# Keys pass of a linear-attention block: products one group later, three shared PSUM banks, sums folded at the end of a batch

## What is computed

```
q, k, v = xn Wq, xn Wk, xn Wv                       16 heads of 32
pq, pk  = exp(u.omega - |u|^2/2 - max(u.omega)) / sqrt(128) + 1e-6     u = scaled q or k, 128 features
kv      = sum over the rows of a batch of pk^T v     per head 128 x 32
z       = sum over the rows of a batch of pk         per head 128
out     = (pq kv) / (pq z) Wo
```

## Time and profile before

| | |
|---|---|
| median of 3 runs | 3785.38 us (3782.58 to 3794.86) |
| the profiled execution's own time | 3801.29 us |
| its span | 3799.5 us |
| granted TensorE clock, mean | 0.968 |
| busy: PE, PEld | 3564.6 us (94%), 3134.4 us (82%) |
| busy: DVE, ACT, POOL | 2196.7 us (58%), 1838.1 us (48%), 1416.3 us (37%) |
| keys pass | 0 to 984 us |
| attend pass | 984 to about 2270 us |
| feed-forward pass | to the end |

### The profile page before, as it was taken

How to read it: one execution, slowest core, us unless ns; L and a number is a source line. 1 busy time by engine, 2 the same in 40 slices (tenths; PEclk the granted TensorE clock), 3 DMA queues, 4 the chain that set the end, 5 groups by cost and what they waited for, 6 DMA issues and landing times. The chain is left out here.

```text
span 3799.5 us, 74203 instructions
## 1 busy us (share of the span) xinstructions
PE 3564.6 (94%) x27634; PEld 3134.4 (82%) x27634; DVE 2196.7 (58%) x3304; ACT 1838.1 (48%) x3944; POOL 1416.3 (37%) x954
## 2 busy tenths in 40 slices
PE   7989988898599999999999968999999999999998
PEld 6777777777488888888888857898898889998897
DVE  5777776677477777877878744333333333333332
ACT  5767766676355555655656534323223222333322
POOL 2544544454344444544445431222222222222222
PEclk9999999999699999999999988999999999999999
DMA  2221232212323232222332324111111111111111
GB/s 95 100 91 67 86 104 85 85 67 90 106 86 102 91 97 94 93 91 92 96 97 92 99 68 145 44 44 44 44 44 44 44 44 44 44 44 44 44 45 49
DMA packets 162443, 283.82 MB, mean 75 GB/s; under 512 B 23696, under 2 KB 52880, under 8 KB 161168
## 3 DMA queue, kind: packets, MB, share of 16 engines
q1 hardware_dynamic: 162192, 280.42, 21.8%
HBM read 166.08 MB, written 114.29 MB: 74 GB/s over the span
## 5 line engine op out<-in xcount | busy, mean ns | idle before, releaser
L1444 DVE TENSOR_TENSOR ffn_hT_lo<-ffn_hid,ffn_hT_hi 128x512 fp32r<-128x512 f32 x256 | 334.3, 1334 | 492.5 <-ACT ffn_hT_hi L1420 492.5
L96 PE MATMUL ffn_hidden<-ffn_yT_hi,ffn_wa_hi 128*128 128x256 f32 x2048 | 573.5, 280 | 11.9 <-DVE ffn_yT_lo L1440 11.9
L96 PE MATMUL ffn_hidden<-ffn_yT_hi,ffn_wa_lo 128*128 128x256 f32 x2048 | 573.6, 280 | 0.0
L96 PE MATMUL ffn_hidden<-ffn_yT_lo,ffn_wa_hi 128*128 128x256 f32 x2048 | 572.6, 280 | 0.0
L1411 ACT ACTIVATE ffn_hid<-ffn_hidden,ffn_bias 128x256 f32<-128x256 f32 x512 | 213.7, 468 | 669.0 <-PE ffn_hidden L96 646.3
L232 POOL TENSOR_TENSOR ffn_n_rstd<-ffn_n_base,ffn_n_power 128x2 f32<-128x2 f32 x32 | 22.5, 702 | 1072.6 <-DVE ffn_n_negmean L227 1072.6
L96 PE MATMUL ffn_result<-ffn_wb_hi,ffn_hT_hi 128*128 128x512 f32 x1024 | 412.0, 402 | 2.4 <-DVE ffn_hT_lo L1444 2.2
L96 PE MATMUL ffn_result<-ffn_wb_hi,ffn_hT_lo 128*128 128x512 f32 x1024 | 404.5, 395 | 0.0
L96 PE MATMUL ffn_result<-ffn_wb_lo,ffn_hT_hi 128*128 128x512 f32 x1024 | 404.2, 395 | 0.0
L96 PEld LDWEIGHTS ffn_hidden<-ffn_yT_hi,ffn_wa_hi 128*128 128x128 f32 x2048 | 384.9, 188 | 20.9 <-DVE ffn_yT_lo L1440 12.2
L96 PEld LDWEIGHTS ffn_hidden<-ffn_yT_lo,ffn_wa_hi 128*128 128x128 f32 x2048 | 385.2, 188 | 8.9
(11 more groups left out here) (229 smaller groups left out, 10112.3 us busy)
## 6 DMA issues: line engine op xcount, KB each, us to landing
attend_uq<-u_d SPq DMA_DIRECT2D x33, 512.0 KB, 3.6
ffn_y_in<-y_d SPq DMA_DIRECT2D x33, 512.0 KB, 3.7
keys_xin<-in_L_attn_x_dram SPq DMA_DIRECT2D x32, 512.0 KB, 5.6
xn_d<-keys_xn SPq DMA_DIRECT2D x32, 512.0 KB, 4.9
xT_d<-keys_xT_whole SPq DMA_DIRECT2D x32, 512.0 KB, 2.7
u_d<-keys_uq SPq DMA_DIRECT2D x32, 512.0 KB, 3.5
attend_xTf<-xT_d SPq DMA_DIRECT2D x32, 512.0 KB, 5.4
r_d<-attend_gate SPq DMA_DIRECT2D x32, 512.0 KB, 2.8
```

The source lines that it names most:

```text
L96: last = pe.matmul(out, stationary[a], moving[b], start=start and n == 0, stop=stop and n == len(TERMS) - 1)
L1444: dve.tensor_tensor(hT[n % HB].lo[:, :, :], hid[n % 2][:, :, :], f32(hT[n % HB].hi[:, :, :]), ALU.subtract).then_inc(h_ready[n % HB], 1)
```

## The change

1. **Ring.** dense0, dense1 and kv go; three banks, ring0 to ring2, serve k, q, v and kv in a fixed rotation.
2. **One group later.** kv of a group runs in the body of the next group, between the dense jobs.
3. **xT in two buffers**, so turn_x of g + 2 no longer waits for the dense jobs of g + 1.
4. **Folding.** The float32 fold of kv and z is done in the keys pass, in the body after a batch's last group: 16 matmuls each (before 8 for kv and 16 for z), both into the bank turn, with an ACT copy after each; the next turn_x waits for the second. DRAM holds 256 KB of kv and 8 KB of z for a batch. The last addition of z goes to a tile of its own, z_all.
5. **The attend pass** loads the folded sums in two loads, and its PE, DVE, ACT, POOL and SP tables lose z and change places a little.

```diff
-        xT = Pair(mem, ctx, "xT", [P, NC, GT])
+        xT = [Pair(mem, ctx, f"xT{n}", [P, NC, GT]) for n in range(2)]
-        dense = [Bank(mem, ctx, f"dense{t}") for t in range(TG)]
-        turn = Bank(mem, ctx, "turn")
-        kv = Bank(mem, ctx, "kv")
+        ring = [ctx.enter_context(mem.psum_tensor(f"ring{n}", [P, W], FP32)) for n in range(3)]
+        k_bank, q_bank, v_bank = (ring[1], ring[0]), (ring[2], ring[1]), (ring[2], ring[1])
+        kv_bank = (ring[0], ring[2], ring[1], ring[0])
...
-        PE_BODY = [("proj", 0, 0), ("k", 0, 1), ("k", 1, 1), ("q", 0, 1), ("proj", 1, 0), ("turn_k", 0, 1),
-                   ("q", 1, 1), ("v", 0, 1), ("turn_k", 1, 1), ("kv", 0, 0), ("v", 1, 1), ("kv", 1, 0), ("kv", 2, 0),
-                   ("turn_x", 0, 2), ("kv", 3, 0), ("turn_x", 1, 2)]
+        PE_BODY = [("kv", 0, -1), ("proj", 0, 0), ("k", 0, 1), ("kv", 1, -1), ("k", 1, 1), ("kv", 2, -1), ("q", 0, 1),
+                   ("proj", 1, 0), ("turn_k", 0, 1), ("kv", 3, -1), ("q", 1, 1), ("turn_k", 1, 1), ("v", 0, 1),
+                   ("fold", 0, -1), ("fold", 1, -1), ("turn_x", 0, 2), ("v", 1, 1), ("turn_x", 1, 2)]
...
+        DVE_BODY = [("top", 0, 0), ("kv", 0, -1), ("stats", 0, 2), ("kv", 1, -1), ("kv", 2, -1), ("top", 1, 0),
+                    ("turn_k", 0, 1), ("pk", 0, 0), ("kv", 3, -1), ("pk", 1, 0), ("turn_k", 1, 1), ("sq", 0, 1),
+                    ("pk", 2, 0), ("sq", 1, 1), ("pk", 3, 0), ("pk", 4, 0), ("turn_x", 0, 2), ("pk", 5, 0),
+                    ("pk", 6, 0), ("v_out", 0, 1), ("v_out", 1, 1), ("turn_x", 1, 2), ("pk", 7, 0)]
+        ACT_BODY = [("k", 0, 1), ("exp", 0, 0), ("exp", 1, 0), ("exp", 2, 0), ("exp", 3, 0), ("hi", 0, 0),
+                    ("k", 1, 1), ("hi", 1, 0), ("norm", 0, 2), ("turn_k", 0, 1), ("hi", 2, 0), ("hi", 3, 0),
+                    ("q", 0, 1), ("exp", 4, 0), ("q", 1, 1), ("turn_k", 1, 1), ("exp", 5, 0), ("fold", 0, -1),
+                    ("hi", 4, 0), ("exp", 6, 0), ("fold", 1, -1), ("hi", 5, 0), ("turn_x", 0, 2), ("v_out", 0, 1),
+                    ("hi", 6, 0), ("exp", 7, 0), ("v_out", 1, 1), ("turn_x", 1, 2), ("hi", 7, 0)]
+        POOL_BODY = [("whole", 0, 1), ("stats", 0, 2), ("z", 0, 0), ("z", 1, 0), ("z", 2, 0), ("z", 3, 0),
+                     ("z", 4, 0), ("z", 5, 0), ("z", 6, 0), ("z", 7, 0)]
+        SP_BODY = [("x", 0, 2), ("q", 1, 1), ("sums", 0, -1), ("whole", 0, 1), ("norm", 0, 2)]
...
+                    pe.wait_ge(x_split, 2 * g + 2)
+                    if job == "k":
+                        bank, full = k_bank[n], k_full[n]
+                        if n == 0:
+                            wait(pe, v_free[1], g)
...
+                            pe.wait_ge(kv_added, NC * (g - 2) + 1)
...
+                if job == "fold" and n == 0:
+                    pe.wait_ge(fold_made, 4)
+                    pe.wait_ge(kv_added, NC * g + NC)
+                    pe.wait_ge(k_split, min(2 * g + 6, 2 * G) if isinstance(g, int) else 2 * g + 6)
+                    for h in range(H):
+                        last = pe.matmul(turn[:, h * KD:(h + 1) * KD], kv_sum[:, h // HC, h % HC * M:(h % HC + 1) * M],
+                                         fold[:, h % 2, :], start=True, stop=True)
+                    last.then_inc(folded, 1)
+                if job == "fold" and n == 1:
+                    pe.wait_ge(z_added[1], NC * g + NC)
+                    pe.wait_ge(fold_out, 2 * b + 1)
```

More of the change, by code:

```diff
@@ L404, in _ @@
             norm.init(pool)
+            pool.memset(ones[:, :], 1.0).then_inc(fold_made, 1)
+            pool.memset(fold[:, :, :], 0.0).then_inc(fold_made, 1)
+            pool.wait_ge(ident_made, 2)
+            pool.wait_ge(fold_made, 2)
+            for a in range(2):
+                half = slice(a * 2 * KD, (a + 1) * 2 * KD)
+                at = a * 2 * KD
+                pool.tensor_tensor(fold[half, a, :], ident[half, at:at + KD], ident[half, at + KD:at + 2 * KD], ALU.add)\
+                    .then_inc(fold_made, 1)
+            pool.wait_ge(fold_made, 4)
             def do(job, n, g, b, i):
@@ L439, in do @@
                     act.wait_ge(norm.ready, g + 1)
-                    wait(act, turn.full, 4 * g - 2)
+                    wait(act, x_turned, 2 * g)
                     wait(act, xn_stored, 16 * g)
@@ L553, in _ @@
             pe.wait_ge(ident_made, 2)
-            pe.transpose(kv.t[:, 0:P], om4[:, :], ident[:, :]).then_inc(omega_turned, 1)
+            pe.transpose(turn[:, 0:P], om4[:, :], ident[:, :]).then_inc(omega_turned, 1)
             pe.wait_ge(omega_ready, 1)
             def do(job, n, g, b, i):
-                if job in ("turn_x", "turn_k"):
-                    src, fill = (xn, 4 * g + n) if job == "turn_x" else (uk, 4 * g + 2 + n)
-                    if job == "turn_x":
-                        pe.wait_ge(xn_ready, TG * g + TG)
-                    else:
-                        for t in range(TG):
-                            pe.wait_ge(dense[t].free, 3 * g + 1)
-                    wait(pe, turn.free, fill)
+                if job == "turn_x":
+                    pe.wait_ge(xn_ready, TG * g + TG)
+                    if n == 0:
+                        wait(pe, k_split, 2 * g)
+                        if i == 2 % GB:
+                            wait(pe, fold_out, 2 * b)
+                    else:
+                        pe.wait_ge(x_split, 2 * g + 1)
@@ new lines, in do @@
+                    last.then_inc(x_turned, 1)
+                if job == "turn_k":
+                    for t in range(TG):
+                        pe.wait_ge(k_free[t], g + 1)
+                    pe.wait_ge(x_split, 2 * g + 2)
+                    wait(pe, k_split, 2 * g + n)
+                    for c in range(2):
+                        for t in range(TG):
+                            last = pe.transpose(turn[:, c * GT + t * P:c * GT + (t + 1) * P],
+                                                uk[:, t, (2 * n + c) * P:(2 * n + c + 1) * P], ident[:, :])
+                    last.then_inc(k_turned, 1)
@@ L577, in do @@
+                    if job == "q":
+                        bank, full = q_bank[n], q_full[n]
+                        if isinstance(g, int) and g < 2:
+                            wait(pe, (v_free[0], k_free[0])[n], g + n)
+                        else:
+                            pe.wait_ge(kv_added, NC * (g - 2) + 2 + n)
+                    if job == "v":
+                        bank, full = v_bank[n], v_full[n]
+                        pe.wait_ge(q_free[n], g + 1)
                     for c in range(NC):
-                        last = product(pe, dense[n].t[:, :], xT[:, c, n * P:(n + 1) * P], w[job][:, c, :],
+                        last = product(pe, bank[:, :], xT[i % 2][:, c, n * P:(n + 1) * P], w[job][:, c, :],
@@ L579, in do @@
                                        start=c == 0, stop=c == NC - 1)
-                    last.then_inc(dense[n].full, 1)
+                    last.then_inc(full, 1)
                 if job == "proj":
-                    pe.wait_ge(turn.free, 4 * g + 4)
+                    pe.wait_ge(k_split, 2 * g + 2)
                     wait(pe, e_ready[1 - n], NC * g + NC if n == 1 else NC * g)
@@ L602, in do @@
                             for s in range(2):
-                                last = pe.matmul(kv.t[:, cols], v[i % 2][:, t, (2 * n + q) * P:(2 * n + q + 1) * P],
+                                last = pe.matmul(kv_bank[n][:, cols], v[i % 2][:, t, (2 * n + q) * P:(2 * n + q + 1) * P],
                                                  pk[t][:, n, cols][s], start=t == 0 and s == 0,
                                                  stop=t == TG - 1 and s == 1)
-                    last.then_inc(kv.full, 1)
+                    last.then_inc(kv_full, 1)
+                if job == "fold" and n == 0:
+                    pe.wait_ge(fold_made, 4)
[5 more added lines that the diff above has]
+                    last.then_inc(folded, 1)
+                if job == "fold" and n == 1:
+                    pe.wait_ge(z_added[1], NC * g + NC)
+                    pe.wait_ge(fold_out, 2 * b + 1)
+                    for h in range(H):
+                        last = pe.matmul(turn[:, 2 * h:2 * h + 2], z_all[:, h // HC, h % HC * M:(h % HC + 1) * M],
+                                         ones[:, :], start=True, stop=True)
+                    last.then_inc(folded, 1)
             run(pe, do, PE_BODY)
@@ L634, in attend_pass @@
         ident = sb("ident", [P, P])
-        ones = sb("ones", [P, 2])
         mask = sb("mask", [P, NC])
```

292 lines of the change are left out of this document (134 added, 158 removed).

## The result

**Slower by 1.2%: 3834.0 us (3830.8 to 3836.1, 4 runs) against 3787.5 before (4 runs), a ratio of 1.012 (1.0101 to 1.014).** That is clear of the noise, if small. Forecast were 3764 and a range up to 3800. The profiled execution has a span of 3830.6 us, 31.1 over the one before.

| us | keys pass | attend pass | feed-forward |
|---|---|---|---|
| before | 986.9 | 1299.8 | 1512.9 |
| after | 1066.7 | 1249.7 | 1514.2 |
| difference | +79.8 | -50.1 | +1.3 |

The account below looks back on a forecast made before the run. PE's (TensorE's) queue sets the time. Steady groups -15, folds +46, last fold +13, tail -9, last store -2, loop boundaries -12, attend pass -42: -21, put on the median, 3764 us; 8-in-10 range 3706 to 3800.

Parts of the forecast that it names:

- the sum: Whole kernel: all terms added, -21 us, put on the median of 3785.38 to give 3764.
- Fold: Keys-pass bodies with a fold: 33.9 us, +6.5 over the 27.4 period, seven times, +46 us.
- 25.55 + 8.55: Keys-pass body with a fold: PE's group without waits, 25.55 us, plus PE time of two folds and hand-overs, given as 8.6.
- a fold much longer than 3.6: Keys pass: named sign that the prediction is wrong altogether; 16 code matmuls of a fold were to take 3.6 us.
- R2: Keys pass, POOL's whole goes ahead of DVE's pk 7: period 29.7, +31 us, 3816; chance 0.15.
- Boundaries: Jumps of the keys-pass loop: smaller stores shorten PE's stops and the slow clock behind, -12 us (bounds -3 and -15).
- the lesser case (-3): Jumps of the keys-pass loop: if store traffic had no part in the stops, the term would be -3, the sum -12.
- Steady group: Keys pass: period 27.4 us, 0.5 less, 30 groups give -15; waits 1.1 at second turn_x, 0.8 at k 0.
- The four pk that meet a z: Steady group on DVE: four pk jobs meeting POOL's z lose 0.66 to 0.95 us each, 3.0 in all.
- Attend pass: Attend pass: two z sums and one kv fold of 1.80 us go per batch, 5.4 in seven, 3.6 in first, -42.
- Last fold, tail and store: End of keys pass: last fold +13 us (bounds 8 and 16), tail -9 (bounds -4 and -12), smaller last store -2.
- Start of the pass: Start of the keys pass: no term of its own in the sum.

Follow-up runs that it names:

- experiment 6: New keys pass (ring, products one group later, two xT buffers) without folds, with old stores and old attend pass, against the kernel before: 0.9977, 3792.8 us.
- experiment 8: Keys-pass loop written out, on the new keys pass without folds and old attend pass (0.9914, 3762.2 us) and on the kernel before (0.996, 3772.3 us).
- experiment 7: Other job places on DVE and POOL: changed kernel 1.0029 of before, 3806.6 us; new keys pass without folds, old attend pass 0.9881, 3750.3 us.
- experiment 2: Changed kernel with the second fold moved behind the next transpose and value product: 1.0067 of the kernel before, 3821.2 us.
- experiment 1: Changed kernel with one matmul instead of 16 in each of the two folds: 0.9933 of the kernel before, 3772.6 us.

## Why the prediction was wrong

Against the profiled execution the sum said -21, and +31 came: 52 us to find.

- **Fold, the step that failed.** "A body with a fold is then 33.9, +6.5": right for the matmuls and hand-overs (6.9 with wide ones; the sum's own terms, 25.55 + 8.55, give 34.1, +6.7), but I took the durations of the earlier trace rows for any such matmul, without asking what the clock does when twice 32 passes come together. Measured 12.4, the second fold 6.96 for 3.6, and "a fold much longer than 3.6" was the prediction's own sign of being wrong; 7 x 5.9 = 41 of the 52. The traces of before had the hint that I did not follow: a sum of 16 there lasts 1.95 and has full clock, but in the attend pass of before the clock falls to 0.50 for about 3 us after some of them (1336 to 1339, 2104 to 2107). No rival had the clock in it; R2, the slower side, was a lock.
- **Boundaries.** I put -12, on the idea that the large stores made the stops long. There are five now instead of four, of 6.9 for 7.4 in the mean: 34.4 for 29.7, +5. That is 17 of the 52. What I called the lesser case (-3) was nearer; experiments 6 and 8 show that traffic has 0.5 us of a stop at most, and the jump the rest.
- **Steady group.** -0.3 for -0.5, and the places and sizes of both waits as laid out: 30 x 0.2 = 6. The four pk that meet a z lose 3.1 us in all (239.60 to 248.80 in the trace), where I had laid out 3.0. This part of the method held: jobs laid on two queues by durations from rows gave 27.4 for 27.61, and experiment 7, drawn up the same way, 26.2 for 26.14.
- **Attend pass.** -42 forecast, -50 in the two profiles. In the four other profiles with the old attend pass and its loop (experiments 6, 7 and 8) it took 1289 to 1297, so the execution of before was slow there by some 5, and the saving is about 45. A batch takes 148.4 where it took 155.3 (154.5 in experiment 6), 6 to 7 less for the 5.4 forecast; the falls of the clock behind its sums, which went with them, would explain the rest, but that was not tried.
- **Last fold, tail and store.** +2 forecast; from the last group's first transpose of x to the attend pass are 80.7 us, before 74.3 (912.58 to 986.87): +6.
- **Start of the pass.** Costed at nothing; the first transpose of the fourth group stands at 91.8, before at 100.8: -9. Which of the new places does it was not tried.

Sum: 41 + 17 + 6 - 8 + 4 - 9 = 51 for 52. The fold alone puts the time past the forecast's range; that the last four leave only -7 together is luck.

That the waits named by the profile were really removed, and the time still rose, is the point of the case: 63.7 us of waits for additions stood for 0.3 us a group, since DVE's next job stood ready to be late, and the work moved on PE was priced by itself and not by what it does to its neighbours.

## What to carry to other kernels

Before narrow float32 matmuls are moved into a stream of wide ones, look at the granted clock around those that the trace already has, and price the wide work behind them at half clock too; a control with the same PE time in wide matmuls tells the two costs apart in one run. A stop without a releaser at a loop's jump is worth an unrolled copy of that loop before anything else is tuned: here 30 to 39 us in one pass by the profiles, 15 to 24 of the whole by the ratios. And when a wait goes, lay out the next one on the waited-for engine: often the order of its jobs gives more (38 us here) than the new buffers that made it possible (8 us).

## What the runs showed that was not expected

- The clock can fall late: in three of seven bodies behind a fold of 3.7 us, in the wide matmuls that follow (experiment 2), and after 2 us of idling with two tiny folds as well (experiment 1).
- Narrow float32 matmuls put between wide ones cost their full time (0.67 for 0.23 and 0.45), at either level of the clock (1.28 at the lower).
- Code that is shorter in the keys pass changed the stops of the attend pass, whose own code was the same. PE's waits there that nothing released (total, times, longest), first of the change, then of experiment 1 with one of its jumps:

```profile
PE attend_feat L1196 <- issue: 11.6, 5, 3.0
```

```profile
PE attend_feat L1196 <- issue: 27.5, 10, 3.9
```

```profile
1305.76 0.33 PE L1196 MATMUL attend_feat<-attend_omegaT_hi,attend_qT_hi 32*128 32x128 f32 x4 [2.63 <-issue]
...
1309.22 0.48 PE L1196 MATMUL attend_feat<-attend_omegaT_hi,attend_qT_hi 32*128 32x128 f32 x4 [2.90 <-issue]
```

Ten stops instead of five, 15.9 us more, and the clock behind them: this is the attend pass of 1267.1 for 1249.7. Only 30 matmuls a fold had been taken out ahead of it. The ten stand in five pairs, 3.5 to 4.4 us apart and about 152 us from pair to pair: each jump stops the engine twice, where in the change it stops it once. So where a loop's code lies seems to decide how often its jump stops the engine; no run moved the code and nothing else. It also means that a difference of some 15 us between two versions of such a kernel can be this alone.
